# Gated two-layer unit on one core: first-stage rows added into x by the gather, the layer norm's scaling moved to ScalarE, statistics three tiles ahead

## The reference

```python
x = x + tanh(g_xattn[0]) * L0_xattn(layernorm(x), ids, ctx, ctx, ctx)    # each row goes to one of 4 experts (by token id)
x = x + tanh(g_ffn[0])   * L0_ffn(layernorm(x), w_gate, w_up, w_down)    # gated MLP, hidden size 2048, quantized
x = x + tanh(g_xattn[1]) * L1_xattn(layernorm(x), ctx, ctx, gamma)       # attention against the context
x = x + tanh(g_ffn[1])   * L1_ffn(layernorm(x), ...)                     # 64 routed experts, top 6, and a shared one

# L0_ffn: every linear layer quantizes its input in blocks of 32 columns
amax  = max(abs(block)); scale = 2 ** (floor(log2(amax)) - 2)
q_act = clip(round_to_small_float(x / scale), -7.5, 7.5) * scale
out   = mx_linear(silu(mx_linear(h, w_gate)) * mx_linear(h, w_up), w_down)
```

## Time and profile before

| | |
|---|---|
| median of 3 runs | 1251.91 us (1250.02 to 1252.6) |
| the profiled execution's own time | 1252.29 us |
| its span, first to last instruction | 1250.6 us |
| busy over the span | PE 82%, DVE 62%, POOL 53%, ACT 31% |
| stage 1, 2, then the rest | about 282, 279 and 690 us |

### The profile page before, as it was taken

One profiled execution on the slowest core, in us unless ns is written; L12 is line 12 of the kernel. 1 busy time (PEld: TensorE's weight loads), 2 busy tenths in 40 slices (PEclk: granted clock), 3 DMA queues, 4 the chain that ended last, 5 costly groups with the idle time before them and its releaser, 6 DMA issues. The chain is left out here.

```text
span 1250.6 us, 14274 instructions
## 1 busy us (share of the span) xinstructions
PE 1031.3 (82%) x4404; PEld 487.5 (39%) x4404; DVE 777.4 (62%) x1233; ACT 393.6 (31%) x781; POOL 660.9 (53%) x550
## 2 busy tenths in 40 slices
PE   5677777684687778867999998899689999999980
PEld 3333334331333333333444444433145555555530
DVE  6899999515789999955777776679612222222220
ACT  4233333231223333325666664412111111111110
POOL 5654565305877777746766665023334554554540
PEclk8988888797889999988999998979689999999995
DMA  7443331001210000005000001732599999999647
GB/s 253 144 143 118 101 121 65 18 34 34 68 34 0 0 0 0 0 3 200 26 18 26 18 1 57 276 96 81 174 350 336 339 341 339 343 340 340 130 61 145
DMA packets 64140, 161.61 MB, mean 129 GB/s; under 512 B 9888, under 2 KB 10032, under 8 KB 63568
## 3 DMA queue, kind: packets, MB, share of 16 engines
q1 hardware_dynamic: 49488, 120.74, 27.4%
q0 software_dynamic: 14592, 40.12, 13.6%
HBM read 129.54 MB, written 35.48 MB: 132 GB/s over the span
## 5 line engine op out<-in xcount | busy, mean ns | idle before, releaser
L1033 POOL TENSOR_TENSOR ARENA<-ARENA 128x512 f32<-128x512 f32 x128 | 134.1, 1069 | 62.9 <-DVE ARENA L1059 62.9
L872 PE MATMUL PS<-SLAB,ARENA 128*128 128x512 bf16 x512 | 119.3, 383 | 21.2 <-DVE ARENA L797 20.5
L1576 POOL DMA_INDIRECT out<-ARENA,idx x32 | 45.9, 1434 | 135.4 <-DVE ARENA L1687 130.6
L1687 DVE COPY ARENA<-PS 96x512 f32<-96x512 f32 x64 | 41.1, 682 | 93.9 <-PE PS L1622 93.9
L1144 ACT ACTIVATE ARENA<-PS,ARENA 128x512 f32<-128x512 f32 x128 | 86.8, 683 | 23.8 <-DVE ARENA L1053 20.6
L531 PE MATMUL PS<-CT,ARENA 128*128 x152 | 91.6, 758 | 2.8 <-issue 1.9
L1652 ACT ACTIVATE ARENA<-PS 96x192 f32<-96x192 f32 x64 | 20.9, 327 | 228.3 <-PE PS L1605 228.3
L1605 PE MATMUL PS<-SLAB,ARENA 128*96 128x384 f32 x240 | 83.0, 499 | 0.0
L1053 DVE TENSOR_REDUCE ARENA<-PS 128x2 f32<-128x1024 f32 x64 | 78.2, 1222 | 7.2 <-PE PS L1105 7.1
L1105 PE MATMUL PS<-ARENA 64*128 64x512 f32 x256 | 74.7, 663 | 8.5 <-DVE ARENA L1047 4.8
L872 PEld LDWEIGHTS PS<-SLAB,ARENA 128*128 128x128 bf16 x512 | 48.5, 99 | 84.0 <-issue 21.6
(11 more groups left out here) (235 smaller groups left out, 2033.1 us busy)
## 6 DMA issues: line engine op xcount, KB each, us to landing
SLAB<-in_L_ffn_w_gate SPq DMA_DIRECT2D x30, 384.0 KB, 7.8
SLAB<-in_L_ffn_w_up SPq DMA_DIRECT2D x30, 384.0 KB, 9.3
X<-in_L_ffn_w_down SPq DMA_DIRECT2D x14, 768.0 KB, 6.9
SLAB<-in_L_ffn_w_down SPq DMA_DIRECT2D x10, 768.0 KB, 6.9
CT<-in_L_ffn_w_gate SPq DMA_DIRECT2D x16, 384.0 KB, 9.7
CT<-in_L_ffn_w_up SPq DMA_DIRECT2D x16, 384.0 KB, 11.6
slot_out<-ARENA SPq DMA_DIRECT2D x19, 256.0 KB, 2.0
X<-in_ctx SPq DMA_DIRECT2D x4, 1024.0 KB, 8.8
```

What stands on the lines that cost most here:

```text
L872: last = pe.matmul(bank(b), QT[:, par, k * P:(k + 1) * P], w[:, k, c * D:(c + 1) * D], start=(k == 0), stop=(k == KD - 1))
L1033: last = pool.tensor_tensor(prob[:, s % 4, h, :], prob[:, s % 4, h, :], rec[:, s % 4, h:h + 1].to_broadcast([P, D]), ALU.mult)
```

## The change

ACT works out `tgate` before stage 1's first slot instead of after its last, and `y(j)` multiplies by the first gate while it copies. The gather of stage 2 then adds the rows straight into X (`compute_op=ALU.add`), so L770 disappears. `deviation` makes one value more, -mean * rstd, on POOL, and the scaling of L780 becomes one ScalarE instruction, `normalise_h`, which writes hn (now two buffers). Statistics are taken three tiles ahead, where they were two ahead. All loops of the stage are written out, and `stand` is dropped from it. Nothing in the later stages changes; the two sums of the experts stay.

```diff
 # stage 1, ScalarE
-                    act.activation(ysb[:, j % 2, :], bank(4 + j % 2), ACT.Copy).then_inc(y_out, 1)
+                    act.activation(ysb[:, j % 2, :], bank(4 + j % 2), ACT.Copy, scale=tgate[:, 0:1]).then_inc(y_out, 1)
...
+                act.wait_ge(g_in, 48)
+                own.link(act.activation(tgate[:, 0:4], gates[:, :], ACT.Tanh))
+                own.link(act.activation(tgate[:, 4:5], tgate[:, 1:2], ACT.Copy, scale=gam[:, 0:1]))
+                own.link(act.activation(tgate[:, 5:6], tgate[:, 2:3], ACT.Copy, scale=float(4 ** A_SHIFT)))
                 normal_h(0)
...
 # stage 2, POOL
-                def deviation(i, par):
+                def deviation(i):
+                    r = i % 4
                     pool.wait_ge(x1_ready, i + 1)
-                    stand(pool)
-                    own.link(pool.tensor_scalar(rs1[:, par:par + 1], mv1[:, par, 1:2], EPS, None, ALU.add))
-                    pool.tensor_tensor(rs1[:, par:par + 1], rs1[:, par:par + 1], neg_half[:, 0:1], ALU.pow).then_inc(rstd1_ready, 1)
+                    need(pool, hn_ready, i - 3)
+                    own.link(pool.tensor_scalar(rs1[:, r, 0:1], mv1[:, r, 1:2], EPS, None, ALU.add))
+                    own.link(pool.tensor_tensor(rs1[:, r, 0:1], rs1[:, r, 0:1], neg_half[:, 0:1], ALU.pow))
+                    pool.tensor_scalar(rs1[:, r, 1:2], mv1[:, r, 0:1], rs1[:, r, 0:1], -1.0, ALU.mult, ALU.mult).then_inc(rstd1_ready, 1)
...
-                        pool.indirect_dma_start(yg[:, i, :], None, slot_out,
-                                                bass.IndirectOffsetOnAxis(ap=slot[:, i:i + 1], axis=0)).then_inc(yg_in[i % 4], 16)
+                        pool.indirect_dma_start(X[:, i, :], None, slot_out, bass.IndirectOffsetOnAxis(ap=slot[:, i:i + 1], axis=0),
+                                                compute_op=ALU.add).then_inc(yg_in[i % 4], 16)
                 gather_four(0)
-                deviation(0, 0)
+                deviation(0)
+                deviation(1)
                 normal_h(0)
                 back_h(0, 0)
-                deviation(1, 1)
+                deviation(2)
                 normal_h(1)
...
 # stage 2, VectorE
-                def enter(i, r, count):
-                    dve.wait_ge(yg_in[r], count)
-                    need(dve, rstd1_ready, i - 1)
-                    own.link(dve.scalar_tensor_tensor(out=one(X, i), in0=one(yg, i), scalar=tgate[:, 0:1], in1=one(X, i),
-                                                      op0=ALU.mult, op1=ALU.add), plain=True)
+                def enter(i):
+                    dve.wait_ge(yg_in[i % 4], 16 * (i // 4) + 16)
+                    need(dve, rstd1_ready, i - 3)
+                    own.link(dve.bn_stats(st1[:, i % 4, :], X[:, i, :]))
+                    dve.bn_aggr(mv1[:, i % 4, :], st1[:, i % 4, :]).then_inc(x1_ready, 1)
...
                 def measure_h(i, par):
-                    dve.wait_ge(rstd1_ready, i + 1)
+                    dve.wait_ge(hn_ready, i + 1)
-                    own.link(dve.tensor_scalar(hn, one(X, i), mv1[:, par, 0:1], rs1[:, par:par + 1], ALU.subtract, ALU.mult))
-                    own.link(dve.tensor_reduce(hmax, blocks(hn), AX.X, ALU.max, apply_absolute_value=True))
+                    own.link(dve.tensor_reduce(hmax, blocks(hn[:, par, :]), AX.X, ALU.max, apply_absolute_value=True))
...
+                for i in range(AHEAD):
+                    enter(i)
                 for i in range(2):
-                    enter(i, i, 16)
                     measure_h(i, i)
                     cast_h(i)
...
-                    if live(i, 2):
-                        enter(i + 2, ...)
+                    if live(i, AHEAD):
+                        enter(i + AHEAD)
...
 # stage 2, ScalarE
+                def normalise_h(i):
+                    act.wait_ge(rstd1_ready, i + 1)
+                    need(act, hy_ready, i - 1)
+                    act.activation(hn[:, i % 2, :], X[:, i, :], ACT.Identity, scale=rs1[:, i % 4, 0:1],
+                                   bias=rs1[:, i % 4, 1:2]).then_inc(hn_ready, 1)
...
                     if live(i, -1):
                         it(i - 1, 0)
+                    if live(i, 2):
+                        normalise_h(i + 2)
```

More of the change, by code:

```diff
@@ L847, in step @@
                         cast_h(i + 2)
[L849 to L854 removed]
+                for i in range(NT + 2):
                     step(i, i % 2)
```

58 lines of the change are left out of this document (20 added, 38 removed).

## The result

The changed kernel took **1220.57 us** (median of 4 runs, 1219.71 to 1222.35), the kernel before 1250.97 (4 runs, 1249.9 to 1252.6): a ratio of 0.9758 [0.974, 0.9776], 30.4 us less. The forecast was 1231 with a range of 1221 to 1244, so the result lies just under the range: the sign and the loop that was walked were right, the size was 10.4 us short. The profiled execution's span fell from 1250.6 to 1220.6 us.

A forecast was written before the change was run, and what follows sets the result against it. DVE was taken as nearest its limit, in a 15.60 us loop through DVE and POOL, with TensorE a second floor. -21.2 - 3.4 + 3.4 + 0.4 + 0.1 = -20.7; 1252.3 - 20.7 - 0.4 = 1231 us, range 1221 to 1244.

The forecast's parts named there:

- The loop and its period: Stage 2 steady tiles, walked from cast_i through DVE's step and POOL's normal_i: period 13.25 us, 2.35 less than 15.60.
- B: Stage 2: DVE and POOL mesh better and TensorE binds at 12.1 us; ten intervals give -35, total 1221; chance 0.1.
- D: Stage 2: hn arrives late from ACT, every step stays 15.5 us, total within 0.2% of 1252; chance 0.04.
- Writing the loops out I cost at nothing beside the 0.10: Stage 2 loops: no gain from writing them out, except 0.10 us where a gap before L820 shrinks to a link.
- the steady term: Nine steady intervals of stage 2, each 2.35 us shorter: -21.2 us.
- Step 13: Tenth interval of stage 2, without enter and deviation: falls from 15.5 to TensorE's 12.1 us, -3.4.
- Steps 14 to 17, 0: Last steps of stage 2, with neither changed part in them before or after: no change, 0 us.
- The gathers and the start: Stage 2 up to step 4: +3.4 us for steps 1 to 3 with costlier gather issues, +0.4 for step 0.
- rival E: Gathers of stage 2: the adding transfer lands late, after some 13 us, total about 1257, slower; chance 0.05.
- rival C: Stage 2: POOL's small instructions wait on DVE, loop about 14.3 us, -11 in all, total 1241; chance 0.18.
- Stage 1: y(j) with its scale costs +0.1 us in the last slots; the tanh, in ACT's idle time, is taken as 0.
- Later stages: 0: Stages after stage 2, which the change leaves alone: no change in time, 0 us.

The follow-up runs named there:

- deviation-late kernel: Changed kernel with POOL's deviation(i+3) moved from ahead of normal_i(i,0) to the end of the step, behind normal_i(i,1): 1231.15 us, ratio 0.9839.
- the filler: Kernel before with 11 transposes of the identity, into an unread bank, in the idle time ahead of the first shared_down product: 1243.81 us, ratio 0.9956.

## Why the prediction was right, and where it was wrong

**The loop and its period.** Right. The period closed through `cast_i`, DVE's step and `normal_i`, the steps came out equal, and the two deleted operations gave 2.20 a tile where the walk gave 2.25. The deleted durations add up to 3.1. Neither PE nor a late hn took over: rivals B and D didn't happen, though TensorE is nearer than I put it (busy 130.3 of 140.5 us). That the time is almost B's 1221 is a coincidence: B needed steps of 12.1. Two slips of the walk: 7.25 + 5.98 is 13.23, which I wrote as 13.25, and 3.83 + 12.1 puts TensorE's last piece at 15.9, not 15.6, with 0.3 us to spare.

**"Writing the loops out I cost at nothing beside the 0.10".** Mis-sized: loops 0.27 and stands 0.21 a step, 0.48 together. I took the interval of 15.50 for one outside the loop, but it ends at the `leave` that stands at the head of step 14, and nearly all of it is step 13, the last in the loop; it says nothing of the loop's price. The missing 0.38 a step, less the 0.05 a step that the two large parts together brought short of the walk, is over nine steps the 3.0 by which the steady term was short.

**Step 13.** -3.1 for -3.4: the step fell to 12.36, not 12.1, with TensorE busy 95% of it.

**Steps 14 to 17, 0.** -1.7 measured. 1.3 of it is the last interval, 9.28 to 7.96, and nearly all of that is the last down product, 6.19 to 4.96 us at another granted clock. The interval was 7.61 to 9.15 in the other versions of the changed kernel, and 7.61 in the kernel before with ten reductions behind stage 2, so it isn't the change's doing.

**The gathers and the start.** +6.1 for +3.8. The addition's price was 10.7, more than the 5.8 in three steps and the 2.1 at the start, since an issue costs 0.6 more instead of 0.48, the landing at the start takes 5.5 instead of 3.6, and `cast_i` fell beside `normal_h` in two steps; the rest of the change gave back 4.6. That landings are hidden from step 1 on was right; rival E needed 13 us, and 5.8 was the longest.

**Small instructions on POOL (rival C).** Didn't happen in the order as changed (0.22, 0.60, 0.26). It did when `deviation` was moved: 0.94.

**Stage 1.** Right: +0.3, the tanh in idle time.

**"Later stages: 0".** The step that failed, -7.4 us, four fifths of the 9.3 by which the span was missed (another 1.3 of the 10.4 in the median is that the profiled execution of the changed kernel lay 1.8 above its median, not 0.4). The argument that untouched work takes untouched time left out that the same work can be granted another clock, 0.50 or 1.00 at this product. The row of a matmul group at 0.50 to 0.60 after 1.72 us of idle time was there to be read. Without it the change is -22.6, to be set against -20.7: 1229 for 1231; without the last down product's clock as well it is -21.3.

That this is so close is partly luck, since 3.0 too little in the steady steps stands against 2.3 too little for gathers and start. Luck also decided on which side of 1221 the time fell: in the long form the changed kernel would have taken about 1228 (an estimate: its later stages at the 689.3 us of the deviation-late kernel instead of 681.7).

Shown: that the 7 us are the clock at this product and just behind it (the filler). Open: what picks the form. It isn't the start time; the work ahead of it is the same in both, and the same program shows both. What goes with it is where an earlier stretch of low clock lies. The kernel before is long in 50 of 56 runs by their times, the one with its loops written out short in all ten; why a kernel leans one way isn't shown. The Trainium skill (TensorE: Matmul & The Clock Gate, "Part 1: The HAM clock gate") says that the gate watches the engine on a beat of its own that a kernel's start doesn't reset, so that where a transition comes depends on how the matmuls fall on it. By that rule two kernels alike up to a fraction of a microsecond may differ, as 790.41 and 790.55 do here; the windows at 0.57 and 0.79 agree with such a shift, but no run shows the gate itself.

## What to carry to other kernels

Find the loop that closes after one period and walk it with the new order; the time of a deleted operation that was waiting for a shared port goes to whatever waits there next, so price pairs of deletions together, not one by one. Price a transfer that computes by its issue and landing on each queue, and look at its gain and its cost in separate stretches: here the adding gather gained 7.5 us in the steady steps and lost 9.0 ahead of them, until the gathers were spread. Compare totals of two kernels only after the untouched stages have been subtracted, and where the clock falls to half in a long matmul group behind an idle time, a microsecond of spare matmuls ahead of it may be worth seven.

## What the runs showed of the hardware

- An indirect gather that adds into SBUF: 1.54 to 1.56 us to issue and 5.0 to 5.8 to land, a plain one of the same 128 rows 0.95 and 3.4 to 4.0.
- A group of 16 matmuls of 128x512 in f32 took 8.50 us at 2.4 GHz and 14.8 when the clock fell in it; 11 small transposes in the idle time ahead of it (1.36 us) kept it at 8.50 in all three profiles that had them. In the long form the clock fell in it behind 1.72 us of idle time.
- Writing loops out was worth 0.27 us per step of 15.6; five `stand`s with two plain links cost 0.21 on 12.9.
- A DVE tensor_scalar on 16 columns lasted 0.17 us alone, 1.25 beside one POOL instruction, and 3.65 right behind four adding gathers, where two POOL instructions follow each other.
